# Sixteen-column products for the halves of exponentials and maxima, and the maximum ahead of the merged rows

## The reference

```python
r = concat([node[src], node[dst], edge]) @ Wr.T + br
k, v = r @ Wk.T + bk, r @ Wv.T + bv          # 8 heads of 64
a = sum(q[dst] * k, axis=-1) * 0.125         # a score for each edge and head
amax = segment_max(a, dst)
ae = exp(a - amax[dst])
attn = ae / segment_sum(ae, dst)[dst]
out = segment_sum(v * attn, dst)             # one row for each node
```

## Time and profile before

| | |
|---|---|
| three runs | 1850.69, 1852.33, 1859.62 us, median 1852.33 |
| the profiled execution | 1861.11 us, its span in the profile 1859.4 us |
| busy over the span | PE 1625.0 us (87%), DVE 1301.8 (70%), ACT 1026.1 (55%), POOL 698.6 (38%) |
| the edge part | about 266 to 1424 us of the span |
| granted TensorE clock | 1.00 from 400 to 1200 us; 0.938 over the span |
| bytes | 300.29 MB by DMA, mean 162 GB/s |

### The profile page before, as it was taken

One profiled execution on the slowest core, in us unless ns is written; L12 is line 12 of the kernel. 1 busy time (PEld: TensorE's weight loads), 2 busy tenths in 40 slices (PEclk: granted clock), 3 DMA queues, 4 the chain that ended last, 5 costly groups with the idle time before them and its releaser, 6 DMA issues. The chain is left out here.

```text
span 1859.4 us, 26827 instructions
## 1 busy us (share of the span) xinstructions
PE 1625.0 (87%) x7160; PEld 1189.9 (64%) x7162; DVE 1301.8 (70%) x3259; ACT 1026.1 (55%) x3674; POOL 698.6 (38%) x723
## 2 busy tenths in 40 slices
PE   7989979999999999999999999999992777888523
PEld 6867767777777777777777777777772333444311
DVE  5875728788877888778878788788774445332688
ACT  3982225777677776777677776777664334200011
POOL 0001224555555555555555555555542000000033
PEclk9989989999999999999999999999996788999855
DMA  5664327566656666566665666566652433000001
GB/s 179 204 224 157 123 87 229 190 203 205 220 196 191 207 209 220 192 198 206 220 207 193 207 211 223 195 208 208 203 181 101 142 102 136 0 1 1 23 12 44
DMA packets 129671, 300.29 MB, mean 162 GB/s; under 512 B 29088, under 2 KB 50727, under 8 KB 129522
## 3 DMA queue, kind: packets, MB, share of 16 engines
q0 software_dynamic: 63600, 180.17, 28.7%
q1 hardware_dynamic: 60738, 107.59, 18.7%
q10 hardware_dynamic: 5184, 10.81, 1.5%
HBM read 271.40 MB, written 66.58 MB: 182 GB/s over the span
## 5 line engine op out<-in xcount | busy, mean ns | idle before, releaser
L1193 ACT ACTIVATE wv<-vv,expd 128x64 f32<-128x64 f32 x1256 | 315.2, 333 | 0.0
L1205 ACT ACTIVATE old<-old,expd 128x64 f32<-128x64 f32 x1256 | 307.8, 333 | 0.0
L1140 POOL DMA_INDIRECT merge<-new,put_id x157 | 159.9, 1019 | 374.5 <-DVE new L1357 341.3
L1401 PE MATMUL psK<-M_hi,efT_hi 128*128 128x512 f32 x628 | 253.2, 403 | 6.3 <-ACT efT_hi L1166 6.3
L1401 PE MATMUL psV<-M_hi,efT_hi 128*128 128x512 f32 x628 | 255.8, 407 | 0.0
L1402 PE MATMUL psK<-M_lo,efT_hi 128*128 128x512 f32 x628 | 249.5, 397 | 0.0
L1402 PE MATMUL psV<-M_lo,efT_hi 128*128 128x512 f32 x628 | 249.5, 397 | 0.0
L1314 DVE TENSOR_TENSOR wv_lo<-wv,wv_hi 128x512 fp32r<-128x512 f32 x157 | 108.9, 693 | 196.2 <-ACT wv_hi L1198 190.5
L1111 POOL DMA_INDIRECT kv<-kv_table,src_id x157 | 164.3, 1047 | 74.9 <-issue 30.8
L1182 ACT ACTIVATE expd<-diff 128x32 f32<-128x32 f32 (+1 forms) x79 | 18.1, 229 | 310.4 <-DVE diff L1338 310.4
L1111 POOL DMA_INDIRECT qc<-q_table,dst_id x157 | 155.4, 990 | 53.7 <-issue 46.9
(11 more groups left out here) (271 smaller groups left out, 3310.1 us busy)
## 6 DMA issues: line engine op xcount, KB each, us to landing
efT<-in_ef_turned_dram SPq DMA_DIRECT2D x78, 512.0 KB, 6.7
merge<-empty ACTq DMA_DIRECT2D x4, 2640.0 KB, 9.7
rows<-merge SPq DMA_DIRECT2D x40, 264.0 KB, 3.5
row_block<-dst_rows POOLq DMA_DIRECT2D x13, 768.0 KB, 5.9
dst_line<-dst_rows SPq DMA_DIRECT2D x78, 128.0 KB, 3.5
end_line<-end_rows SPq DMA_DIRECT2D x78, 128.0 KB, 5.3
kv_table<-kv_out SPq DMA_DIRECT2D x10, 512.0 KB, 3.3
raw<-in_L_gnn_Wr_dram SPq DMA_DIRECT2D x12, 256.0 KB, 5.4
```

What stands on the lines that cost most here:

```text
L1140: pool.indirect_dma_start(out=merge[2 * (p % 2) + u][:, :], out_offset=bass.IndirectOffsetOnAxis(ap=put_id[:, t:t + 1], axis=0), in_=new[p ...
L1193: act.activation(wv[:, u, h * DH:(h + 1) * DH], vv[p % 2][:, u, h * DH:(h + 1) * DH], ACT.Copy, scale=expd[p % 2][:, u, 0, h:h + 1]).then_ ...
L1205: act.activation(rows, rows, ACT.Copy, scale=expd[p % 2][:, u, 1, h:h + 1]).then_inc(old_scaled, 1)
L1401: pe.matmul(out[:, :], efT_hi[b][:, u, c, :], Me_hi[:, c, col:col + D], start=c == 0, stop=False)
```

## The change

The high and the low part of the turned maxima, and those of the exponentials, are written side by side into one tile (`run_parts`, `exp_parts`, each 2 parts of 8 columns), and one product of 16 columns takes the place of the two of 8 columns. Their two halves lie apart in PSUM, and VectorE adds them by a `tensor_reduce` over the parts (`top_sum`, `sum_den`). On VectorE `maximum(p-1)` is moved ahead of `scale_den(p-2)` and `merge_rows(p-2)`; `exp_low_part(p-2)` and both `wv_low_part` are moved behind `scan(p-1)`. On ScalarE the high part of the exponentials (`weights_high`) is moved behind `weigh_v` of the first tile.

```diff
-        runs_hi = sb("runs_hi", [P, 2, H], F32R)
-        runs_lo = sb("runs_lo", [P, 2, H], F32R)
+        run_parts = sb("run_parts", [P, 2, 2, H], F32R)
+        top_sum = sb("top_sum", [P, 2, H])
...
-        den = psO[:, 2 * P:2 * P + 2 * H].rearrange("p (u h) -> p u h", h=H)
+        den = psO[:, 2 * P:2 * P + 4 * H].rearrange("p (u s h) -> p u s h", s=2, h=H)
         turned_s = psT[:, 0:2 * H].rearrange("p (u h) -> p u h", h=H)
-        top = psT[:, 2 * H:4 * H].rearrange("p (u h) -> p u h", h=H)
+        top = psT[:, 2 * H:6 * H].rearrange("p (u s h) -> p u s h", s=2, h=H)
...
+            def weights_high(p):
+                n = tiles_of(p)
                 act.wait_ge(exp_ready, exp_at(p))
-                act.activation(exp_hi[p % 2][:, 0:n, :], expd[p % 2][:, 0:n, 0, :], ACT.Copy).then_inc(exp_ready, 1)
+                act.activation(exp_parts[p % 2][:, 0:n, 0, :], expd[p % 2][:, 0:n, 0, :], ACT.Copy).then_inc(exp_ready, 1)
...
                     weights(p - 1)
                     weigh_v(2 * p - 2)
+                    weights_high(p - 1)
...
-                dve.tensor_tensor(new[b][:, 0:n, ROW:TROW], old[b][:, 0:n, ROW:TROW], top[:, 0:n, :],
+                dve.tensor_reduce(top_sum[:, 0:n, :], top[:, 0:n, :, :].rearrange("p u s h -> p u h s"),
+                                  AX.X, ALU.add).then_inc(max_step, 1)
+                dve.wait_ge(max_step, top_at(p))
+                dve.tensor_tensor(new[b][:, 0:n, ROW:TROW], old[b][:, 0:n, ROW:TROW], top_sum[:, 0:n, :],
                                   ALU.max).then_inc(max_step, 1)
...
                     dve.wait_ge(summed, t + 1)
+                    if u == n - 1:
+                        dve.tensor_reduce(sum_den[:, 0:n, :], den[:, 0:n, :, :].rearrange("p u s h -> p u h s"),
+                                          AX.X, ALU.add).then_inc(den_step, 1)
                     dve.wait_ge(old_scaled, H * (t + 1))
                     dve.tensor_tensor(new[b][:, u, 0:D], psS[u][:, :], old[b][:, u, 0:D], ALU.add).then_inc(new_ready, 1)
-                dve.wait_ge(den_step, scaled_at(p))
-                dve.tensor_tensor(new[b][:, 0:n, D:ROW], den[:, 0:n, :], old_den[:, 0:n, :], ALU.add).then_inc(den_step, 1)
+                dve.wait_ge(den_step, summed_at(p))
+                dve.tensor_tensor(new[b][:, 0:n, D:ROW], sum_den[:, 0:n, :], old_den[:, 0:n, :], ALU.add).then_inc(den_step, 1)
...
                 if last:
                     add_v(2 * p - 2)
-                if older:
-                    exp_low_part(p - 2)
-                    wv_low_part(2 * p - 4)
                 if last and tiles_of(p - 1) == 2:
                     add_v(2 * p - 1)
                 if last:
                     row_one_hots(p - 1)
                     scan(p - 1)
-                if older and tiles_of(p - 2) == 2:
-                    wv_low_part(2 * p - 3)
+                if older:
+                    exp_low_part(p - 2)
+                    for t in range(2 * p - 4, 2 * p - 4 + tiles_of(p - 2)):
+                        wv_low_part(t)
...
                 if p + 1 < PAIRS:
                     low_part(p + 1)
+                if last:
+                    maximum(p - 1)
                 if older:
                     scale_den(p - 2)
                     merge_rows(p - 2)
-                if last:
-                    maximum(p - 1)
...
-                    pe.matmul(top[:, u, :], from_end[:, u, :], runs_hi[:, u, :], start=True, stop=False)
-                    pe.matmul(top[:, u, :], from_end[:, u, :], runs_lo[:, u, :], start=False, stop=True).then_inc(top_done, 1)
+                    pe.matmul(top[:, u, :, :], from_end[:, u, :], run_parts[:, u, :, :], start=True, stop=True).then_inc(top_done, 1)
...
-                    pe.matmul(den[:, u, :], same[p % 2][:, u, :], exp_hi[p % 2][:, u, :], start=True, stop=False)
-                    pe.matmul(den[:, u, :], same[p % 2][:, u, :], exp_lo[p % 2][:, u, :], start=False, stop=True)
+                    pe.matmul(den[:, u, :, :], same[p % 2][:, u, :], exp_parts[p % 2][:, u, :, :], start=True, stop=True)
```

More of the change, by code:

```diff
@@ L1019, in edges @@
         runs = sb("runs", [H, 2 * P])
-        runs_hi = sb("runs_hi", [P, 2, H], F32R)
-        runs_lo = sb("runs_lo", [P, 2, H], F32R)
+        run_parts = sb("run_parts", [P, 2, 2, H], F32R)
+        top_sum = sb("top_sum", [P, 2, H])
         diff = two("diff", [P, 2, 2, H])
         expd = two("expd", [P, 2, 2, H])
-        exp_hi = two("exp_hi", [P, 2, H], F32R)
-        exp_lo = two("exp_lo", [P, 2, H], F32R)
+        exp_parts = two("exp_parts", [P, 2, 2, H], F32R)
         vv = two("vv", [P, 2, D])
@@ L1030, in edges @@
         old_den = sb("old_den", [P, 2, H])
+        sum_den = sb("sum_den", [P, 2, H])
         psK = [bank("psK0"), bank("psK1")]
@@ L1063, in score_at, with top_at, diff_at, scaled_at @@
             return 2 * t + 2
+        def top_at(p):
+            return 4 * p + 1
         def newmax_at(p):
+            return 4 * p + 2
+        def diff_at(p):
+            return 4 * p + 4
+        def scaled_at(p):
             return 3 * p + 1
-        def diff_at(p):
+        def summed_at(p):
+            return 3 * p + 2
+        def den_at(p):
             return 3 * p + 3
[L1072 to L1077, removed]
         def exp_at(p):
@@ L1172, in copy_runs @@
                     act.wait_ge(top_done, 2 * p)
-                act.activation(runs_hi[:, 0:n, :], turned_s[:, 0:n, :], ACT.Copy).then_inc(runs_copied, 1)
+                act.activation(run_parts[:, 0:n, 0, :], turned_s[:, 0:n, :], ACT.Copy).then_inc(runs_copied, 1)
             def weights(p):
@@ L1289, in runs_low_part @@
                     dve.wait_ge(top_done, 2 * p)
-                dve.tensor_tensor(runs_lo[:, 0:n, :], turned_s[:, 0:n, :], runs_hi[:, 0:n, :].bitcast(F32),
+                dve.tensor_tensor(run_parts[:, 0:n, 1, :], turned_s[:, 0:n, :], run_parts[:, 0:n, 0, :].bitcast(F32),
                                   ALU.subtract).then_inc(runs_low, 1)
@@ L1297, in exp_low_part @@
                     dve.wait_ge(summed, 2 * (p - 1))
-                dve.tensor_tensor(exp_lo[b][:, 0:n, :], expd[b][:, 0:n, 0, :], exp_hi[b][:, 0:n, :].bitcast(F32),
+                dve.tensor_tensor(exp_parts[b][:, 0:n, 1, :], expd[b][:, 0:n, 0, :], exp_parts[b][:, 0:n, 0, :].bitcast(F32),
                                   ALU.subtract).then_inc(exp_low, 1)
```

## The result

The changed kernel takes 1938.57 us in the median of four runs (1934.35 to 1941.98), the kernel before 1855.97 us in four runs beside it (1850.69 to 1863.52): a ratio of 1.0441, with a 95% interval from 1.0391 to 1.0491. Forecast were 1787 us and a range that ended at 1858. The change is slower by 83 us, and the forecast fell. The kernel before took 1855 us also beside e1 to e4 and beside e13 to e16, but 2035 us beside e5 to e8, 1938 beside e9 to e12, 1928 beside e17 and 1957 beside e18, each time with a lower granted clock over the run (0.90 in the first of these and 0.92 to 0.93 in the others, against 0.94).

The account below looks back on a forecast made before the run. The prediction took a 14.22 us ScalarE-VectorE ring plus late old rows as the bound; afterwards a ring through memory, 9.46 + L (4.1) = 13.56 us. Saving 0.84 us over 77 turns, 65 us, gave 1787 us off the median; range 1752 to 1858.

Parts of the forecast that it names:

- L: Landing time of the last old-row read after its issue by GpSimd: forecast 4.1 us, 6.6 in the median before.
- TensorE: Four of eight small products go each turn, saving 0.44 us; TensorE's own list falls from 13.62 to 13.18 us.
- VectorE and ScalarE's ring: Runs to exponential: merged rows (1.36 us) leave, a 0.19 us reduce enters; 14.22 us in the quiet turn becomes 13.05.
- two 13.05 us rings: The ScalarE-VectorE ring and a second way over the weighed values' low part, each forecast at 13.05 us a turn.
- The ring through memory: Reduce, store, old-row reads after the stores, next maximum: a new ring of 9.46 + L us.
- slower rival: The ring through memory decides from L = 4.98; at 5.4 plus 32 us, at 6.6 plus 125 us; chance 0.20.
- 6.47 to the last read's issue: Ring-through-memory term: time from a turn's first store to GpSimd's issue of the last old read, kept at 6.47 us.
- move into the empty slices: SyncE's lines and efT (768 KB, 1.9 us) move into the turn's nearly idle first slices, so L falls from 6.6 us.
- TensorE waits for the denominators: Rival: the sort of scores waits for VectorE in every turn, 13.9 to 14.0 us a turn, 1814 us; chance 0.08.
- Old rows at the floor: Rival: L is 3.4 to 3.7 us, TensorE's 13.18 us sets the turn, saving 97 us, 1755 us; chance 0.24.

Follow-up runs that it names:

- e1: Changed kernel with the two index lines (dst_line, end_line) loaded for the first two pairs only: 1859.2 us, 1.002 of the kernel before.
- e4: Changed kernel with SyncE's line loads, and efT behind them, also waiting for the turn's first key addition: 2068.0 us, 1.1145 of the kernel before.
- e13: The changed kernel run again, unaltered: 1940.4 us, 1.0463 of the kernel before.
- e16: Changed kernel, GpSimd order old, key-value, query, line loads held until VectorE begins the scores, low parts waiting for both high parts: 1911.1 us, 1.0302.
- e5: Changed kernel with the maximum put back behind the merged rows, the rest of the change kept: 1871.6 us.
- e8: Changed kernel with GpSimd's order old, key-value, query, and line loads held back by the second addition of keys: 1935.0 us.
- e9: The same kernel as e5, run again (changed kernel, maximum back behind the merged rows): 1873.1 us.
- e12: Changed kernel with VectorE waiting for both high parts of the weighed values before making the low parts, nothing left out: 1867.7 us.
- e17: Changed kernel, GpSimd order unchanged, low parts waiting for both high parts, line loads held until VectorE has begun the scores: 1881.9 us.
- e18: The same kernel as e12, run again (changed kernel, low parts waiting for both high parts): 1866.9 us.
- e6: Kernel before with only the wide products and the two reduces, every order as before: 2030.1 us beside 2034.9, 0.9968.
- e14: Changed kernel with lines loaded for the first two pairs only and low parts waiting for both high parts: 1820.7 us, 0.9812 of the kernel before.
- e7: Kernel before with only the maximum moved ahead of scale_den and merge_rows: 1934.7 us.
- e10: The same kernel as e7, run again (kernel before, only the maximum moved ahead): 1937.7 us.
- e3: Changed kernel with denominators in another PSUM bank and sums ahead of the turning, so the sort waits for no denominators: 1950.1 us, 1.0507.
- e15: Changed kernel with GpSimd's order old, key-value, query and line loads held until VectorE has begun the scores: 1917.8 us, 1.0327.

## Why the prediction was wrong

It forecast one ring in which only L was open, and wrote the other terms down as they stood before. Point by point:

- *TensorE*: right as far as it was seen. One load at each small product, the loads behind the two of the spread 0.11 us apart (1206.49 and 1206.60), and no stall before the spread. Its list of 13.18 us was never the longest, so no run measured it, and e6 gives no price for the products.
- *VectorE and ScalarE's ring*: the reduce took 0.19 us and 0.22 to the next step, the second reduce 0.10 of issue: right. The two 13.05 us rings were never the longest, so no run measured them; with the merged rows left in the ring, e9 has it at 14.57 us, within 0.1 us of 14.22 and the two reduces (0.28).
- *The ring through memory*: the mechanism was right, and it was named as the slower rival, with 0.20. First reduce to store: 2.92 us forecast by its terms, 2.97 measured (they add up to 9.47 + L, not 9.46). L: 4.1 forecast, 3.8 measured, and `efT` at 2.3 us as said. **The step that failed is the term "6.47 to the last read's issue"**: it measured 8.68. Of the 1.96 us by which the turn missed 13.6, these 2.2 are more than all, and L gave 0.3 back.
- *Why that term moved*: `fetch_old` waits for the landing of the stores (`put`), and this wait was not costed, because before it had 1.3 us to spare: landed at 3.9, first old read at 5.2. (Some 0.3 us of that are needed: in the changed kernel the read starts 0.3 us after the landing.) Two parts of the change took more than that. The low parts, moved behind the scan, now lie beside the second store, which takes 1.8 us instead of 1.0; and the lines and `efT`, issued 1.0 to 2.3 us behind the first store, delay its landing. Taking away the lines alone gives 1.1 us of issue (e1), moving the low parts alone 1.2 us (e12), both 1.8 us (e14), and the median turn is then 13.71 us where 13.6 was forecast. The ring itself is closed by the maximum's new place: put back, 66 us return (e5, e9); moved alone, it costs as much as the whole change (e7, e10).
- *It and the lines "move into the empty slices"*: these were not empty for the purpose. In those first microseconds the stores move few bytes, but everything behind them hangs on their landing. The rate of the earlier trace rows shows bytes, not who waits for them.
- *The slower rival* erred in its price as well: it kept the issue at 6.47 and let L decide at 4.98. With L at 3.8 it should not have come true, and the time still came to its side.
- *TensorE waits for the denominators*: the pause is there in each turn, 3.35 us in the one shown, and taking it away gains nothing (e3).
- *Old rows at the floor*: L reached it (3.2 to 3.7 us), and the 97 us did not follow.

## What to carry to other kernels

When an order closes a ring through memory, cost every hop of it, each wait that is satisfied today with its slack beside it; here 1.3 us of slack under a wait of GpSimd decided the forecast. A load that is moved out of one crowd is moved into another: name what is in flight at its new place, and ask whose landing the next issue waits for, not only how many bytes move. An instruction that is moved on one engine can lengthen one of another engine: look at what runs beside it at its new place. The longest new stall of a profile need not be the cause (TensorE's before the sort was not), and taking it away is the cheap way to find out.

## What the runs showed of the hardware

- *GpSimd's transfers beside VectorE.* GpSimd's instruction for a store of 128 rows takes 1.0 us by itself. In the changed kernel the 59 long ones of 310 to 1350 us (1791 ns mean) have `wv_lo` beside them for 672 ns of their first microsecond, the 76 short ones (1017 ns) for 41 ns; with the low parts moved away (e12, e14) all take 1.0 us. What decides is the moment. Where `wv_lo` was under way at the store's start, or began within 0.3 us after it, the store ended 0.88 us after `wv_lo` did: 1.19 us in 62 stores of e10 (`wv_lo` begun 0.4 us before), 1.48 in ten of e15 (0.1 before), 1.80 in 57 of the changed kernel (0.2 after). Where it began 0.4 us after the start or later, the store took 1.0 us (1.1 to 1.2 in four of e15). Reads can be held in the same way: 43 key-value reads of e10 begun 0.1 us after `efT_lo` took 1.93 us instead of 0.95, ending 0.82 us after it.

```profile
809.90 1.93 POOL L1111 DMA_INDIRECT kv<-kv_table,src_id  x1 [0.30 <-issue]
```
```profile
809.79 1.22 DVE L1227 TENSOR_TENSOR efT_lo<-efT,efT_hi 128x1024 fp32r<-128x1024 f32 x1
```

But of the changed kernel's query reads 57 start together with a `wv_lo` and take 0.99 us. The Trainium skill (SBUF — State Buffer, Who interferes with whom) says that a VectorE instruction with two SBUF inputs contends with a GpSimd instruction that reads SBUF, and infers that `tensor_tensor` does not hold up the making of a transfer's descriptors. These runs agree with the first and not with the inference: GpSimd's instruction for a transfer is held, for stores and for reads.
- *Landing of the stores.* Counted from the start of a turn's first store, the second one (270 KB) has landed at 3.7 us where the first load came 1.6 us or more after its own start (e10), at 3.8 with `efT` 1.2 us after it (two turns of e1), at 5.1 with `efT` 0.7 us after it (e14), and at 7.0 in the changed kernel, with lines and `efT` and 0.8 us more of issue. In e16 it landed at 6.4: there the query reads issued just ahead of it in GpSimd's own queue landed at 6.0, and the lines and `efT`, issued 4 to 5.5 us ahead, at 2.0 to 3.4 us; which of them held it was not separated. The Trainium skill (DMA: Bandwidth & Descriptors, Queues, rings and completion order) has each DMA engine take turns between the queues by packets. That a load issued close behind a store delays it goes with this; the size of the delay was not worked out from it.
- *The clock after a stall.* After the 3.35 us in which TensorE stood still the granted clock is low, then full again:

```profile
1195.00:1198.10 3.10, 3.10 (x10) 2.47 (x9) 2.41 (x6) 3.04 (x12) 2.62 (x2) 0.52 0.24 80
1198.10:1203.00 4.90, 4.90 (x24) 3.74 (x23) 3.59 (x6) 4.90 (x18) 2.79 (x4) 1.00 0.79 253
```

The first is the lower of the two levels, 1.2 GHz: loads for products of 512 columns start 0.42 us apart (1195.52 to 1195.94) instead of 0.24. Over 310 to 1350 us the granted clock is 0.95, and VectorE waited 21.9 us in all for key products. A low clock is not needed for a long turn: e15 and e16 have 1.00 over the same stretch and turns of 15.2 us.
